# Hop 0 of a graph kernel: the next unit is turned before the queries' product, and ScalarE copies it before it drains the queries

## The reference

```python
Q = relu(h @ Wq + bq).reshape(n, HEADS, D)
K = (h @ Wk + bk).reshape(n, HEADS, D)
V = (h @ Wv + bv).reshape(n, HEADS, D)
# hop 0
Kj  = relu(K[row] + ef)
msg = norm[:, None, None, None] * einsum('ehi,ehj->ehij', Kj, V[row])
M   = segment_sum(msg, col)
K   = segment_sum(norm[:, None, None] * Kj, col)
# hops 1 and 2
M   = segment_sum(norm * M[row], col)
# after each hop
H   = einsum('nhi,nhij->nhj', Q, M)
```

## Time and profile before

| | |
|---|---|
| median of three runs | 1689.41 us |
| lowest, highest | 1685.13, 1690.41 us |
| the profiled execution, its own time | 1689.98 us |
| its span in the profile | 1687.1 us |
| granted TensorE clock, mean | 0.894 of full speed |

### The profile page before, as it was taken

How to read it: one execution, slowest core, us unless ns; L and a number is a source line. 1 busy time by engine, 2 the same in 40 slices (tenths; PEclk the granted TensorE clock), 3 DMA queues, 4 the chain that set the end, 5 groups by cost and what they waited for, 6 DMA issues and landing times. The chain is left out here.

```text
span 1687.1 us, 21574 instructions
## 1 busy us (share of the span) xinstructions
PE 1292.7 (77%) x5794; PEld 792.3 (47%) x5794; DVE 1434.0 (85%) x2664; ACT 1005.7 (60%) x2692; POOL 1202.7 (71%) x1185
## 2 busy tenths in 40 slices
PE   4888888889899777877854777775778999777771
PEld 3666666566666544544531333332233444454551
DVE  6889988899999759899897999994556987799991
ACT  4998988699999735455443555553555665233330
POOL 7777777777775077777707777774777777777776
PEclk8999999899999869799876989997999999888886
DMA  4455553567665459999876888885345454466640
GB/s 133 104 129 121 127 125 110 142 156 171 166 162 145 115 153 328 298 322 332 289 265 205 296 310 305 301 309 172 97 143 158 143 158 142 131 178 178 172 133 16
DMA packets 281214, 313.79 MB, mean 186 GB/s; under 512 B 169010, under 2 KB 198570, under 8 KB 268551
## 3 DMA queue, kind: packets, MB, share of 16 engines
q1 hardware_dynamic: 224166, 246.39, 47.4%
q0 software_dynamic: 56928, 66.04, 15.3%
HBM read 214.54 MB, written 161.32 MB: 223 GB/s over the span
## 5 line engine op out<-in xcount | busy, mean ns | idle before, releaser
L977 PE MATMUL bank<-product,ident 128*128 128x512 f32 (+1 forms) x800 | 380.5, 632 | 137.0 <-DVE product L1369 137.0
L578 POOL DMA_INDIRECT state<-state_hop,slot_of_src x392 | 394.5, 1006 | 126.1 <-issue 107.3
L749 ACT ACTIVATE bank<-state,norm 128x512 f32<-128x512 f32 x392 | 251.4, 679 | 253.5 <-DMA state<-state_hop,slot_of_src 218.4
L1369 DVE TENSOR_TENSOR product<-bank,queries 128x512 f32<-128x512 f32 x392 | 261.4, 688 | 88.9 <-ACT bank L749 86.9
L977 PEld LDWEIGHTS bank<-product,ident 128*128 128x128 f32 x800 | 159.5, 204 | 356.7 <-issue 181.2
L554 POOL DMA_INDIRECT row_of_src<-node_rows,pos_int x196 | 195.5, 997 | 114.4 <-issue 56.7
L540 POOL DMA_INDIRECT x_edges<-in_x,dst_tiles x196 | 211.2, 1078 | 59.8 <-issue 59.8
L540 POOL DMA_INDIRECT x_edges<-in_x,src_tiles x196 | 201.2, 1027 | 62.7 <-issue 58.8
L594 POOL DMA_INDIRECT out<-rows,dst_out x196 | 194.0, 990 | 59.7 <-issue 57.3
L1367 DVE SCALAR_TENSOR_TENSOR acc<-acc,same_as_before,bank 128x512 f32<-128x512 f32 x196 | 145.3, 742 | 15.5 <-ACT bank L749 14.8
L1153 DVE TENSOR_TENSOR bank<-kv,bank 128x512 f32<-128x512 f32 x196 | 135.2, 690 | 15.2 <-issue 12.7
(11 more groups left out here) (220 smaller groups left out, 2831.7 us busy)
## 6 DMA issues: line engine op xcount, KB each, us to landing
state_hop<-acc SPq DMA_DIRECT2D x98, 1024.0 KB, 4.6
x_nodes<-in_x SPq DMA_DIRECT2D x49, 256.0 KB, 4.1
src_row<-in_src_row SPq DMA_DIRECT2D x49, 256.0 KB, 3.6
out<-out_rows SPq DMA_DIRECT2D x49, 256.0 KB
dst_row<-in_dst_row SPq DMA_DIRECT2D x49, 256.0 KB, 3.8
kv_rows<-kv SPq DMA_DIRECT2D x49, 256.0 KB, 3.5
gg<-head_sums SPq DMA_DIRECT2D x98, 128.0 KB
kv_back<-kv_rows SPq DMA_DIRECT2D x49, 256.0 KB
```

Source lines behind the costliest of these rows:

```text
L578: pool.indirect_dma_start(out=mg[u % 4][:, k, :], out_offset=None, in_=d_m[hop - 1], in_offset=bass.IndirectOffsetOnAxis(ap=sidx[:, t:t + ...
L749: act.activation(pw[t % len(pw)][:, :], mg[u % 4][:, k, :], ACT.Copy, scale=wn12[:, t:t + 1]).then_inc(weighted, 1)
L977: ins = ten.matmul(ph[:, 0:k * D].rearrange("p (c j) -> p c j", j=HD), ident[:, :], part, start=(r == 0), stop=(r == HD - 1))
L1369: vec.tensor_tensor(ihj(pr[m % 2][:, u % 2 * EH + k, :]), ihj(pw[t % len(pw)][:, :]), over_j(Q[:, t, :]), ALU.mult).then_inc(multiplied, 1)
```

## The change

Two blocks move, one on TensorE and one on ScalarE. On TensorE the queries' wait and product leave the block of keys and values and come after the turn of the next unit. On ScalarE the copy of the next unit's turned rows comes after the copy of the values and ahead of the queries' four activations. No instruction, tile, buffer or DMA is added or removed, and each block keeps the waits it had.

```diff
@@ ScalarE
                     act.activation(kvz[u % 3][:, :, D:2 * D], parts[:, :, 1, :], ACT.Copy).then_inc(v_done, 1)
+                u = g - C0
+                if 0 <= u < CU:
+                    act.wait_ge(turned_z, u + 1)
+                    wait(act, q_mm, u - 1)
+                    act.activation(hTz[u % 2][:, :], pTz[:, :], ACT.Copy).then_inc(copied_z, 1)
+                u = g - C0 - 1
+                if 0 <= u < CU:
                     act.wait_ge(q_mm, u + 1)
                     for k in range(EH):
                         t = u * EH + k
                         ins = act.activation(Q[:, t, :], pQz[:, k * D:(k + 1) * D], ACT.Relu, scale=dinv[:, t:t + 1])
                     ins.then_inc(q_done, 1)
-                u = g - C0
-                if 0 <= u < CU:
-                    act.wait_ge(turned_z, u + 1)
-                    wait(act, q_mm, u - 1)
-                    act.activation(hTz[u % 2][:, :], pTz[:, :], ACT.Copy).then_inc(copied_z, 1)
@@ TensorE
                                start=False, stop=True, skip_group_check=True).then_inc(kv_z, 1)
-                    wait(ten, q_done, u)
-                    rows_out(pQz, hTz[u % 2][:, W:2 * W], Wq, 2, EH // 2, q_mm)
                 u = g - C0
                 if 0 <= u < CU:
...
                     ins.then_inc(turned_z, 1)
+                u = g - C0 - 1
+                if 0 <= u < CU:
+                    wait(ten, q_done, u)
+                    rows_out(pQz, hTz[u % 2][:, W:2 * W], Wq, 2, EH // 2, q_mm)
```

## The result

The changed kernel took 1681.33 us (median of nine runs), the kernel before 1688.36 us beside it: ratio 0.9961, 95% interval 0.9944 to 0.9978. That is 7.0 us less, inside the forecast range and 1.3 us above the forecast of 1680.0. The forecast gain was 9.8, so the gain is 2.8 short. The time comes closer than the gain because the forecast was reckoned down from the profiled execution of before, 1689.98 us, and beside the changed kernel the median of before was 1.6 us under that.

A forecast was written before the change was run, and what follows sets the result against it. DVE in hop 0 was taken to bound the kernel, starving 11.6 us at TensorE's low clock; 9.8 of it returned, 1689.98 - 9.8 = 1680.2, given as 1680.0 us, range 1675.5 to 1686.5.

The forecast's parts named there:

- DVE starves only at the low clock: Hop 0 after 626.78: DVE's 11.6 us idle lies where TensorE ran at 1.2 GHz, tick 7.37 against DVE's 5.20.
- The slow tick becomes 6.63: TensorE in hop 0 at 1.2 GHz: turn ahead of queries hides ScalarE's copy, tick 6.63 us, 0.74 less.
- The fast tick becomes about 4.1: Hop 0 at the full clock: ScalarE's copy ahead of the queries' activations cuts the loop from 4.95 to about 4.1 us.
- The loop at the full clock no longer bounds: Hop 0 at full clock: DVE needs 5.20 us a unit, so TensorE waits for DVE; this buys lead, 2.3 us.
- Of 11.6 us, 9.8 come back: DVE's idle time in hop 0 after 626.78: 9.8 of 11.6 us saved, taken between bounds 7.6 and 11.6.
- nothing about the clock changes: Lower bound in hop 0: the low-clock stretches stay as they are, 7.6 us saved.
- no gap left: Upper bound in hop 0: slow stretches shorten until the lead covers them, all 11.6 us come back.
- All behind the stage moves with it: Hop 1 and later: whatever hop 0 gains or loses on DVE moves everything behind it by the same amount.
- The start gives nothing, POOL does not bind but is near: Hop 0: nothing counted before 626.78; POOL's gathers, 5.20 us a unit, cap the gain at 11.4 to 16.9 us.
- The clock turns against it: Rival in hop 0: longer stops per fast tick keep TensorE slow most of the stage, 1695.7 us; chance 0.06.

The follow-up runs named there:

- the kernel of before with a fuller TensorE: Kernel before plus one overwritten 512-column matmul per tick on TensorE, waiting only for DVE: 1680.42 us, ratio 0.9938.
- The single early norms: Changed kernel with the edge norms of units 2 to 5 made singly and one unit later: 1680.80 us, ratio 0.9946 to the kernel before.

## Why the prediction was right, step by step

- *DVE starves only at the low clock.* Right, and shown by the kernel of before with a fuller TensorE.
- *The slow tick becomes 6.63.* It is 6.52. *The fast tick becomes about 4.1.* It is 4.12 where DVE does not hold it. *The loop at the full clock no longer bounds.* Right: TensorE waits for DVE in 26 ticks of 48.
- *Of 11.6 us, 9.8 come back.* DVE's groups from 626.3 us to the end of the stage in the changed kernel, against the earlier trace rows:

```profile
L1157 DVE TENSOR_TENSOR bank<-kv,bank 128x512 f32<-128x512 f32 x184 | 125.9, 684 | 0.7 <-issue 0.7
L1312 DVE TENSOR_TENSOR dinv_of_src<-row_of_src,src_slots 128x8 f32<-128x8 f32 (+1 forms) x23 | 3.7, 160 | 4.3 <-DMA row_of_src<-node_rows,pos_int 4.3
```

The idle time ahead of outer products fell from 12.2 to 0.7, 11.5 us. Of the 4.3 us for rows, 3.1 are the wait at 626 itself; the other 1.2 are new and go off the gain, so 10.3 net in place of 9.8. The rest of the stage's 11.9 is 0.8 us at its start and 0.8 in outer products and sums that took a little less time each. The two bounds were 7.6 ("nothing about the clock changes") and 11.6 ("no gap left"), and half way between them is 9.6, not 9.8. "No gap left" was nearly the case. Long stretches at the low clock became short ones, as forecast, and there were more of them: from 650 us on the longest is 10.2 us in the first profile of the change and 13.7 in the second, 20.5 in before. The stretch of 13.7 cost one gap of 1.06 us. As above, the one profile of before holds more of these gaps than its usual execution seems to, so a forecast worked out from it alone starts too high.
- *All behind the stage moves with it.* Right for hop 1 (its first POOL step 11.7 us earlier), but single gathers of the hops differ by 3 us from one execution to the next. The time fell by 7.0 us, not by the stage's 11.9. By the estimate above, most of the difference is that the one profile of before had a longer stage than usual, with two slow stretches of 20 us; no second profile of it was made, so this stays an estimate. That 1681.33 came within 1.3 us of the forecast is in part luck: the stage's gain in the profiles was larger than the forecast's and what the program kept of it was smaller, and the kernel before was 1.6 us faster than the value that the forecast started from.
- *The start gives nothing, POOL does not bind but is near.* Nearly right: up to the wait at 626 us the stage is 0.8 us shorter, and DVE waited 0.70 and 0.51 us for rows later. POOL is nearer than I had said: I had let DVE end at least 16.6 to 22.1 us after the last gather, and it ends after 21.5. The single early norms moved the wait and not the end.
- *The clock turns against it.* It did not for the whole change, but it is just what happens to TensorE's half alone, with 74 us and not the 5.7 of that rival: I had counted full slow ticks, and not that a stop in each tick can bring the clock down nearly every time.
- *Missed:* ScalarE's value scaling now waits for the edge norm, 22.5 us in 21 ticks against nearly nothing before. TensorE's lead runs into the norms that DVE makes on its way. It is inside the lead and cost nothing.

## What to carry to other kernels

When the busiest engine has gaps only where TensorE's clock is low, compare the serial loop's length at either clock with the busy engine's pace; shortening the loop at the full clock builds lead and pays too (1.8 us in a fall of 20 us here), though TensorE's loop was already faster than DVE there. Reorder both ends of a hand-over together, or test each half: TensorE's half alone made a stop in every tick and cost 74 us, ScalarE's half alone gave as much in the program's time as both. Before a forecast is worked out from one profile, check that its rare events (here two slow stretches of 20 us) are usual. A cheap test of "is it the clock" is to add matmuls where they wait for nothing new; if the program gets faster with more work, it was. A matmul that waits for something in the loop lengthens the loop and tells nothing.

## What the runs showed of the hardware that was not expected

- With a stop of 1.59 us in each tick of 6.75 to 7.3 us, a few longer, TensorE fell to 1.2 GHz in nearly every tick of the stage (mean granted clock 0.72). With two more matmuls in that stop the clock was 1.00 and the tick 5.34 us.
- 392 gathers of the same instruction on POOL summed to between 394.5 and 398.0 us in ten profiles of programs that differ in nothing there.
- On one chip the kernel before took 2078.28 us where its medians elsewhere were 1688.36 to 1689.85.
